# A decoder layer on one core: experts' down matrices split in two halves, a shorter staging ring, a slot table in PSUM, a new order of steps

## What is computed

```
# block 1: gated memory
gate = sigmoid(xn @ Wg + bg);  store = (xn @ Wv) * gate * scale
mem  = smear(store, 0.95)                      # a scan along the sequence
x    = x + (mem * sigmoid(xn @ Wq + bq) * scale) @ Wo
# block 2: attention over a context of 256 rows of 64
kv   = ctx @ W_k.T + b_k
sim  = (xn @ kv) @ kv.T / 16
x    = x + softmax(layernorm(sim) * gamma + beta)
# block 3: one of 8 experts per token, and a shared expert
idx, score = argmax(xn @ router_w), sigmoid(max(xn @ router_w))
for e in range(8): out += where(idx == e, (silu(xs @ gate_w[e]) * (xs @ up_w[e])) @ down_w[e], 0)   # xs = xn * score
x    = x + out + (silu(xn @ sh_gate) * (xn @ sh_up)) @ sh_down
```

## Time and profile before

| | us |
|---|---|
| runs shown | 143.40, 144.98, 147.16; median 144.98 |
| the profiled execution | 144.02, of which the span of the core's instructions 142.3 |
| busy in the span | PE 113.3 (80%), DVE 91.2 (64%), POOL 75.5 (53%), ACT 65.7 (46%) |
| mean granted clock of TensorE | 0.948 |
| DMA | 16.44 MB, mean 116 GB/s |
| chain that ended last | PE 65%, issue 11%, DVE 9%, POOL 4%, DMA 4%, ACT 3% |

### The profile page before, as it was taken

One profiled execution on the slowest core, in us unless ns is written; L12 is line 12 of the kernel. 1 busy time (PEld: TensorE's weight loads), 2 busy tenths in 40 slices (PEclk: granted clock), 3 DMA queues, 4 the chain that ended last, 5 costly groups with the idle time before them and its releaser, 6 DMA issues.

```text
span 142.3 us, 2530 instructions
## 1 busy us (share of the span) xinstructions
PE 113.3 (80%) x679; PEld 93.0 (65%) x679; DVE 91.2 (64%) x279; ACT 65.7 (46%) x169; POOL 75.5 (53%) x110
## 2 busy tenths in 40 slices
PE   0199999999899997968889301989999999999700
PEld 0169699687697894856769101757888888888400
DVE  2673995489999799799468998047554553643100
ACT  3335996936996347662350100034445444444300
POOL 5207069281894376556866992000446646646680
PEclk9999999999999999999999965589999999999985
DMA  4997984917047225002215702933254363243200
GB/s 130 242 277 170 368 264 105 280 60 223 0 134 244 72 72 149 0 7 78 78 39 193 245 0 50 316 126 77 78 89 79 81 91 61 29 48 37 29 1 0
DMA packets 18924, 16.44 MB, mean 116 GB/s; under 512 B 4320, under 2 KB 18656, under 8 KB 18912
## 3 DMA queue, kind: packets, MB, share of 16 engines
q1 hardware_dynamic: 15792, 13.56, 32.2%
q0 software_dynamic: 2544, 2.17, 9.2%
q10 hardware_dynamic: 576, 0.56, 1.1%
HBM read 11.82 MB, written 5.38 MB: 121 GB/s over the span
## 4 chain that ended last, share of the span: by engine, by line
PE 65%; issue 11%; DVE 9%; POOL 4%; DMA 4%; ACT 3%; SPq 1%; POOLq 0%; ACTq 0%
PE bG L876 15%; PE bQ L876 12%; PE bO L957 5%; PE bV L1083 4%; PE bV L876 4%; PE bO L1083 4%; DMA ez<-in_ctx_dram 4%; PE bU L965 3%; PE bV L1032 3%; PE bS L975 2%; POOL x_sorted L436 2%; PE bM L876 2%; PE bT L1054 1%; POOL out_dram L457 1%; PE bU L882 1%
## 5 line engine op out<-in xcount | busy, mean ns | idle before, releaser
L457 POOL DMA_INDIRECT out_dram<-tq,tid x15 | 23.3, 1552 | 29.0 <-DVE tid L846 26.3
L443 POOL TENSOR_TENSOR gu_lo<-stage,gu_hi 128x512 fp32r<-128x512 f32 x16 | 20.1, 1282 | 0.2
L1032 PE MATMUL bV<-shd,xn 128*128 128x256 f32 x32 | 9.5, 450 | 9.1 <-DVE xn L813 9.1
L1032 PEld LDWEIGHTS bV<-shd,xn 128*128 128x128 f32 x32 | 6.9, 225 | 10.5 <-issue 9.5
L436 POOL DMA_INDIRECT x_sorted<-xs,dest x8 | 8.4, 1056 | 5.1 <-issue 3.6
L409 POOL TENSOR_SCALAR vareps<-mv 128x2 f32<-128x2 f32 x8 | 2.0, 248 | 16.4 <-DVE mv L666 16.2
L663 DVE BATCH_NORM_STATS2 bn<-res 128x6 f32<-128x256 f32 x24 | 8.9, 414 | 2.3 <-DMA res<-in_x_dram 2.3
L612 ACT CAST xT_hi<-bT 128x256 fp32r<-128x256 f32 x8 | 2.9, 368 | 13.9 <-PE bT L1054 13.9
L493 ACT CAST gu_hi<-stage 128x512 fp32r<-128x512 f32 x16 | 9.3, 618 | 0.0
L474 ACT ACTIVATE xn<-res,shift,rstd 128x256 f32<-128x256 f32 x14 | 7.7, 596 | 3.5 <-POOL shift L417 3.5
L1083 PE MATMUL bV<-dn,xT 128*128 x32 | 8.3, 383 | 0.6 <-ACT xT L624 0.6
(11 more groups left out here) (190 smaller groups left out, 342.5 us busy)
## 6 DMA issues: line engine op xcount, KB each, us to landing
stage<-in_L_ffn_gate_w_dram SPq DMA_DIRECT2D x8, 256.0 KB, 3.5
stage<-in_L_ffn_up_w_dram SPq DMA_DIRECT2D x8, 256.0 KB, 3.3
dn<-in_L_ffn_down_w_dram SPq DMA_DIRECT2D x8, 256.0 KB, 3.5
xs<-x_sorted SPq DMA_DIRECT2D x15, 136.0 KB, 2.1
res<-in_x_dram SPq DMA_DIRECT2D x4, 256.0 KB, 3.5
out_dram<-res SPq DMA_DIRECT2D x4, 256.0 KB, 2.9
x_sorted<-pad SPq DMA_DIRECT2D x5, 136.0 KB, 2.9
x_sorted<-pad ACTq DMA_DIRECT2D x4, 136.0 KB, 3.0
```

The source lines that it names most:

```text
L443: g.tensor_tensor(units[n][2], stage[:, n % RING], f32(units[n][1]), ALU.subtract).then_inc(unit_lo, 1)
L457: g.indirect_dma_start(out_rows, bass.IndirectOffsetOnAxis(tid[:, s:s + 1], 0), ry[:, s % TILE_RING, :], None, bounds_check=N - 1, oob_is_ ...
L1032: last = T.matmul(psV[:, i, :], hs[:, b % 2, k, i * P:(i + 1) * P], shd[:, k, :], start=(k == 0), stop=(k == KT - 1))
```

## The change

Four things change. (1) `down_w` of each expert becomes a third unit of the ring, split into dn_hi and dn_lo: 29 units instead of 21, eight weight_hi more on ACT and eight weight_lo more on POOL, and no direct loads of dn. In the tile loop the hidden rows are split too (hidden_hi on ACT in place of the copy, hidden_lo new on DVE), and down becomes `product` with six matmuls of 256 columns. (2) RING goes from 6 to 4. (3) Four rows of the slot table (ntile, tile_s, te_f, and offset, formerly in tr_f) lie in a PSUM bank. (4) All four orders are laid out anew. A wait in weight_lo for the table is dropped; it belonged to a unit number that the old list didn't have.

```diff
 POOL_ORDER = """
-    rstd1:0 rstd1:1 rstd1:2 rstd1:3 weight_lo:3 weight_lo:4 sim_eps:0 weight_lo:5 weight_lo:6
-    sim_eps:3 rstd3:2 sim_rstd:3 scale_rows:1 scatter:0 rstd3:3 scatter:1 scale_rows:2 scatter:2
-    scale_rows:3 scatter:3 weight_lo:15 weight_lo:16 weight_lo:17 weight_lo:18 weight_lo:19
+    rstd1:0 rstd1:1 rstd1:2 rstd1:3 weight_lo:3 weight_lo:4 weight_lo:5 weight_lo:6 sim_eps:0
+    sim_eps:3 sim_rstd:3 rstd3:2 scale_rows:1 scatter:0 rstd3:3 weight_lo:23 weight_lo:24 scatter:1
+    scale_rows:2 scatter:2 scale_rows:3 scatter:3 weight_lo:25 weight_lo:26 weight_lo:27
...
     TILE_RING = 2 * KT
     ROUNDS = (NS - 3 - PEEL) // TILE_RING
-    RING = 6
+    RING = 4
     PROJ = 3
 
...
         gu_hi = sb("gu_hi", [P, E, KT, 2 * D], F32R)
         gu_lo = sb("gu_lo", [P, E, KT, 2 * D], F32R)
-        dn = sb("dn", [P, E, KT, D])
+        dn_hi = sb("dn_hi", [P, E, KT, D], F32R)
+        dn_lo = sb("dn_lo", [P, E, KT, D], F32R)
         kvT_all = sb("kvT_all", [C, B, S])
         kv_rows = sb("kv_rows", [P, B, KT, C])
...
-        ntile = sb("ntile", [1, E])
-        tile_s = sb("tile_s", [1, NS])
-        te_f = sb("te_f", [1, NS])
-        before = sb("before", [1, NS])
+        preceding = sb("preceding", [1, NS])
-        hT = xT2[:, :, :, 0:P]
+        hT_hi, hT_lo = xT1_hi[:, :, :, P:2 * P], xT1_lo[:, :, :, P:2 * P]
...
+        spare = 2 * TB * E
+
+        def ps_row(n):
+            nonlocal spare
+            spare += n
+            return bT[0:1, spare - n:spare]
+
+        ntile, tile_s, te_f, offset = ps_row(E), ps_row(NS), ps_row(NS), ps_row(NS)
-        small_in = {n: sem(f"{n}_in") for n in ("wk", "ctx", "bk", "bias", "wo", "gamma", "beta", "rw", "shd", "dn")}
+        small_in = {n: sem(f"{n}_in") for n in ("wk", "ctx", "bk", "bias", "wo", "gamma", "beta", "rw", "shd")}
...
         units += [(rows(w), shw_hi[:, i], shw_lo[:, i]) for i, w in enumerate((sh_gate_w, sh_up_w))]
         for e in range(E):
             units += [(rows(gate_w[e]), gu_hi[:, e, :, 0:D], gu_lo[:, e, :, 0:D]),
-                      (rows(up_w[e]), gu_hi[:, e, :, D:2 * D], gu_lo[:, e, :, D:2 * D])]
+                      (rows(up_w[e]), gu_hi[:, e, :, D:2 * D], gu_lo[:, e, :, D:2 * D]),
+                      (rows(down_w[e]), dn_hi[:, e], dn_lo[:, e])]
         SHARED_LO = 2
-        LAST_AFTER_TABLE = 26
 
         def f32(ap):
             return ap.bitcast(F32)
...
             sp.dma_start(x_sorted[E * REGION:E * REGION + P, :], pad[:, :]).then_inc(padded, 16)
             for n in range(PROJ, len(units)):
                 load_unit(n)
-                if n == PROJ + 1:
+                if n == RING:
                     load("shd", shd[:, :, :], rows(sh_down_w))
-                if n >= RING and (n - RING) // 2 < E and (n - RING) % 2 == 0:
-                    load("dn", dn[:, (n - RING) // 2], rows(down_w[(n - RING) // 2]))
-            for e in range((len(units) - RING + 1) // 2, E):
-                load("dn", dn[:, e], rows(down_w[e]))
 
             def store_base(b):
...
 
             def weight_lo(n):
                 pool.wait_ge(unit_hi, n + 1)
-                if n == LAST_AFTER_TABLE:
-                    pool.wait_ge(table_made, 1)
                 g.tensor_tensor(units[n][2], stage[:, n % RING], f32(units[n][1]), ALU.subtract).then_inc(unit_lo, 1)
 
             steps = {"rstd1": lambda b: rsqrt(LN1, b),
...
-            def hidden_copy(s, r, reused):
+            def hidden_hi(s, r, reused):
-                a.copy(hT[:, r], psH[r][:, :, 0:P]).then_inc(hT_made, 1)
+                a.copy(hT_hi[:, r], psH[r][:, :, 0:P]).then_inc(hT_hi_made, 1)
...
                     dve.wait_ge(table_step, step[0])
 
                 link(v.tensor_tensor(cmp_k[:, :, :], io_k[0:1, :, :], ps_count[0:1, :].unsqueeze(2).to_broadcast([1, E, NT]), ALU.is_lt))
-                link(v.tensor_reduce(ntile[:, :], cmp_k[:, :, :], AX.X, ALU.add))
-                link(v.tensor_tensor_scan(incl[:, :], one_e[:, :], ntile[:, :], 0.0, ALU.mult, ALU.add))
-                link(v.tensor_scalar(tile_s[:, :], io_s[:, :], incl[:, E - 1:E], None, ALU.min))
-
-                link(v.tensor_tensor(cmp_s[:, :, :], tile_s[:, :].unsqueeze(2).to_broadcast([1, NS, E]),
+                link(v.tensor_reduce(ntile, cmp_k[:, :, :], AX.X, ALU.add))
+                link(v.tensor_tensor_scan(incl[:, :], one_e[:, :], ntile, 0.0, ALU.mult, ALU.add))
+                link(v.tensor_scalar(tile_s, io_s[:, :], incl[:, E - 1:E], None, ALU.min))
+
+                link(v.tensor_tensor(cmp_s[:, :, :], tile_s.unsqueeze(2).to_broadcast([1, NS, E]),
                                      incl[:, :].unsqueeze(1).to_broadcast([1, NS, E]), ALU.is_ge))
-                link(v.tensor_reduce(te_f[:, :], cmp_s[:, :, :], AX.X, ALU.add))
-                link(v.tensor_tensor(cmp_s[:, :, :], cmp_s[:, :, :], ntile[:, :].unsqueeze(1).to_broadcast([1, NS, E]), ALU.mult))
-                link(v.tensor_reduce(before[:, :], cmp_s[:, :, :], AX.X, ALU.add))
-                link(v.tensor_tensor(tr_f[:, :], tile_s[:, :], before[:, :], ALU.subtract))
-                link(v.tensor_scalar(tr_f[:, :], tr_f[:, :], float(P), None, ALU.mult))
-                v.tensor_scalar(te[:, :], te_f[:, :], E - 1.0, None, ALU.min)
-                v.scalar_tensor_tensor(tr[:, :], te_f[:, :], float(REGION), tr_f[:, :], ALU.mult, ALU.add).then_inc(table_made, 1)
+                link(v.tensor_reduce(te_f, cmp_s[:, :, :], AX.X, ALU.add))
+                link(v.tensor_tensor(cmp_s[:, :, :], cmp_s[:, :, :], ntile.unsqueeze(1).to_broadcast([1, NS, E]), ALU.mult))
+                link(v.tensor_reduce(preceding[:, :], cmp_s[:, :, :], AX.X, ALU.add))
+                link(v.tensor_tensor(offset, tile_s, preceding[:, :], ALU.subtract))
+                link(v.tensor_scalar(tr_f[:, :], offset, float(P), None, ALU.mult))
+                v.tensor_scalar(te[:, :], te_f, E - 1.0, None, ALU.min)
+                v.scalar_tensor_tensor(tr[:, :], te_f, float(REGION), tr_f[:, :], ALU.mult, ALU.add).then_inc(table_made, 1)
 
             def shared_hidden(b):
...
 
+            def hidden_lo(s, r):
+                dve.wait_ge(hT_hi_made, s + 1)
+                v.tensor_tensor(hT_lo[:, r], psH[r][:, :, 0:P], f32(hT_hi[:, r]), ALU.subtract).then_inc(hT_lo_made, 1)
+
             rows_lo(0, 0, 0)
             rows_lo(1, 1, 1)
             hidden(0, 0)
             rows_lo(2, 0, 2)
             for s in range(PEEL):
                 hidden(s + 1, (s + 1) % 2)
+                hidden_lo(s, s % 2)
                 rows_lo(s + 3, (s + 1) % 2, (s + 3) % TILE_RING)
             with dve.Fori(0, ROUNDS) as i:
                 for j in range(TILE_RING):
                     s = i * TILE_RING + (PEEL + j)
                     r = (PEEL + j) % 2
                     hidden(s + 1, 1 - r)
+                    hidden_lo(s, r)
                     rows_lo(s + 3, 1 - r, (PEEL + j + 3) % TILE_RING)
             for s in range(PEEL + ROUNDS * TILE_RING, NS):
                 if s + 1 < NS:
                     hidden(s + 1, (s + 1) % 2)
+                if s < NS:
+                    hidden_lo(s, s % 2)
                 if s + 3 < NS:
                     rows_lo(s + 3, (s + 1) % 2, (s + 3) % TILE_RING)
...
                 if reused:
-                    pe.wait_ge(hT_made, s - 1)
+                    pe.wait_ge(hT_lo_made, s - 1)
                 for k in range(KT):
                     last = T.transpose(psH[r][:, k, 0:P], rh[:, r, k * P:(k + 1) * P], ident[:, :])
                 last.then_inc(th_done, 1)
 
             def down(s, r, e, reused):
-                pe.wait_ge(hT_made, s + 1)
+                pe.wait_ge(hT_lo_made, s + 1)
                 if reused:
                     pe.wait_ge(y_made, s - 1)
-                for k in range(KT):
-                    last = T.matmul(psY[r][:, 0, :], hT[:, r, k, :], dn[:, e, k, :], start=(k == 0), stop=(k == KT - 1))
-                last.then_inc(down_done, 1)
+                product(psY[r][:, 0, :], [(hT_hi[:, r, k, :], hT_lo[:, r, k, :], dn_hi[:, e, k, :], dn_lo[:, e, k, :])
+                                          for k in range(KT)]).then_inc(down_done, 1)
 
             pe.wait_ge(table_made, 1)
             e = experts(0, NS)
             pe.wait_ge(unit_lo, len(units) - PROJ)
-            pe.wait_ge(small_in["dn"], 16 * E)
             rows_turn(0, 0, 0, 1, False)
             rows_turn(1, 1, 1, 1, False)
             pe.wait_ge(sm["h_made"], B)
```

62 lines of the change are left out of this document (32 added, 30 removed).

## The result

| | before | changed |
|---|---|---|
| median, us | 144.82 (143.4 to 147.16, 4 runs) | 140.61 (139.75 to 140.62, 4 runs) |
| profiled execution, span | 142.3 | 138.5 |
| T, first row transposes | 91.56 | 89.30 |
| from T to the end | 50.7 | 49.2 |

The ratio is 0.9724, 95% interval 0.9656 to 0.9792: faster, but by 4.2 us where I had said 9.5 (144.98 to 135.5), and 0.1 us outside my range. (Ratios here leave disturbed runs out, medians don't, so the two can differ.) T is where PE starts on the first row transposes, in the kernel before with their weight load under the running shared_down (the matmul itself at 91.99). Of the two terms, T came 2.3 us earlier instead of 6.9, and the part behind T is 1.5 us shorter instead of 2.4.

A forecast was written before the change was run, and what follows sets the result against it. Bound: PE idle 9 us behind te, held on DVE by POOL; then POOL's last weight_lo. From 144.02 us: T -6.9, first transposes -0.4, tile loop -2.0, holds and clock +0.8, in sum -8.5: 135.5 us, range 131.5 to 140.5.

The forecast's parts named there:

- The table's rows in PSUM: On DVE ahead of T: te reading PSUM isn't held by POOL's run, 0.2 us instead of 7.93, saving 7.7 us.
- Rival 1: At te on DVE: the stall stays wherever te reads, T 88.8 to 90.6, 139.5 to 141 us; chance 0.12.
- What is late next, POOL: Ahead of T: POOL finishes last, rstd3:3 ends at 65.0 and the last weight_lo at 84.7, so T moves -6.9 us.
- rival 2: In the front: POOL's weight_lo hold kv_mean, centre_kv and residual3 on DVE, 1.3 to 5.1 us, 136 to 140; chance 0.18.
- holds and clock together: Term of +0.8 us for DVE held in longer weight_lo runs and for the clock behind PE's 3.5 us wait.
- Down in two halves: Tile loop: down takes 0.72 us instead of 0.86, -2.0 us over 14 periods; hidden_lo's latency is hidden.
- The 0.4 us for the first transposes: On PE at T: first transposes at full clock, 0.22 us a pair instead of 0.44, twice: -0.4 us.
- POOL's added 10.3 us: Eight more weight_lo at 1.28 us, said to fit in POOL's some 15 us of pauses and charged nothing.
- The own case: The forecast's main case: the stall goes, POOL sets T at 84.7, 135.5 us in all; chance 0.55.
- Rival 3: POOL's front: pauses stay unused, the 10.3 us come on top, T 96.6 and 147.0 us; chance 0.10.
- rival 4: PE-bound front: POOL finishes before PE, T at 81.2, 132 us; chance 0.05.
- What would show it: Signs: te 0.2, last weight_lo at 83 to 88, PE waiting about 3, period 2.55 us; wrong if turn_kv waits.

The follow-up runs named there:

- e1: The kernel before with only the slot table's rows put in PSUM: 140.97 us, ratio 0.9711.
- e5: The changed kernel with only the slot table's rows put back in SBUF: 146.68 us in one run.
- e9: The changed kernel with a probe behind its end: twelve times two scatters, six weight_lo, and te from SBUF at shifted starts; its time says nothing.
- e16: e14 with shared_hidden:0 left out but for two columns: similarity:3's start to rstd3:3's end stayed at 12.9 us; no total time given.
- e3: The changed kernel with sim_scale:3, destination:1 (DVE), softmax_exp:3 and score_tanh:2 (ACT) moved: 140.53 us.
- e8: The changed kernel with the edits of e2 and e3, and destination:0 directly behind sim_stats:3 on DVE: 138.19 us, ratio 0.9546.
- e10: e8 with route:1 back ahead of sim_scale:3 on DVE and destination:0 behind sim_stats:3: 139.65 us, ratio 0.9666.
- e2: The changed kernel with centre_kv reading PSUM and weight_lo:15 waiting for residual3:0, to remove two DVE holds: 138.89 us, ratio 0.9523.
- e7: e1 (down not split, six buffers) with weight_lo:15 to 18 moved from behind scatter:3 into POOL's pauses: 138.55 us.
- e15: The changed kernel with six staging buffers instead of four: 140.35 us, ratio 0.9734.
- e14: e2 with score_tanh:2 moved ahead of weight_hi:25 on ACT: 139.73 us, ratio 0.9528.

## Why the prediction was right or wrong

**The table's rows in PSUM**: right, and shown by e1 (5.1 us at T) with its ratio of 0.971. The reason I gave, a run of POOL instructions holding a DVE instruction that reads SBUF, is shown by the probes, but to the run's end only for a run that closely follows a scatter; without one it was held for one weight_lo. In the new order the rows weren't needed (e5). Rival 1 is out: PSUM ended the hold in all pieces. Its argument from `tr_f` has lost its force with e9: `tr_f` began 0.76 us ahead of the run, between the 0.65 that is held and the 0.87 that isn't, so where it began is enough to explain that it went through.

**What is late next, POOL**: right in kind (PE waits for the last weight_lo at T, with te, ring and DMA in time), wrong in size. The step that failed is "I count 1.5 to 2.3 us earlier, and take 2. Then rstd3:3 ends at 65.0". It ended 3.9 us later than that:
- 2.0 us: I took the way from similarity:3 to rstd3:3 as unchanged. It grew from 10.9 to 12.9 us. In both kernels rstd3:3 starts on POOL right behind scatter:0, scatter:0 waits for destination:0, and this stands on DVE behind sim_stats:3, route:1 and sim_scale:3. New between sim_stats:3 and sim_scale:3 is residual3:2, 1.9 us (58.36 to 60.29). Before (destination:0's end, rstd3:3's start), then after (residual3:2, and the same two):

```profile
61.61 0.17 DVE L780 CAST dest<-dest_f 128x2 uint32<-128x2 f32 x1
...
65.45 0.24 POOL L409 TENSOR_SCALAR vareps<-mv 128x2 f32<-128x2 f32 x1
...
58.53 0.88 DVE L751 SCALAR_TENSOR_TENSOR res<-ez,rsum,res 128x256 f32<-128x256 f32 x2
...
63.53 0.17 DVE L782 CAST dest<-dest_f 128x2 uint32<-128x2 f32 x1
...
67.29 0.24 POOL L413 TENSOR_SCALAR vareps<-mv 128x2 f32<-128x2 f32 x1
```

Counted from the start of similarity:3 (56.14 and 55.95), destination:0 ends after 5.64 us before and 7.75 us after; from there to rstd3:3's start it is 3.67 and 3.59 us. Less work on DVE ahead of similarity:3 didn't shorten it (e16). No run moved residual3:2, so that it alone costs the 2 us is read from the traces and not tested; e3, e8 and e10 moved steps around it, and each time another wait ended last (destination:0 still behind route:1; scale_rows:1 for the score of sequence 1; rstd3:2, 1.89 us for residual3:2). Which exchange would undo it is open: the exponentials that residual3:2 reads ended at 57.84 us, so it couldn't simply go back ahead of sim_stats:3.
- 1.3 us: the holds of rival 2, shown by e2. I had +0.8 for holds and clock together, with up to 5.1.
- 0.5 us: without the holds similarity:3 is 1.5 us earlier than before, not 2. This is less than executions differ by in where their steps lie, so it has no cause shown.

Behind rstd3:3 I had 19.7 us to the last weight_lo; it took 20.4. POOL waited 1.5 us for the score, which followed from half clock on PE, a cost that I had placed behind T alone. The rest of this way was 0.8 us shorter.

**Down in two halves**: right in the period (2.53 against 2.55, down 0.71 against 0.72) and in that nothing else bounds it. Wrong was "in the last tile it is hidden by POOL": PE waited 0.88 and 1.06 us for hidden_lo in the last tiles and the last down ran at half clock. From the start of the last gate_up to that of the last scatter it is 8.5 us (124.73 to 133.26) against 7.8 before (129.25 to 137.03): 0.7 us of the 2.0 lost. The 0.4 us for the first transposes came by half: they took 0.44 and 0.38 us instead of 0.64 and 0.63, and gate_up began 1.5 us behind them instead of 1.7.

**The sum**: -2.3 at T and -1.5 behind it make -3.8 in the span of the profiled executions (-3.4 in their times, 144.02 to 140.61), against -8.5. That POOL's added 10.3 us would hide was right for POOL itself, which still waited for DVE ahead of rstd3:3; their price was the time for which they held DVE. The own case, with rival 2's mechanism inside it, is what happened, at a time that the range missed by 0.1 us: the range had no room for an unpriced 2 us in a step that I took from before as it stood. **Rival 3** (147.0) and **rival 4** (PE as the bound) didn't occur.

**What would show it**: te 0.2 (0.16), unit_lo's last directly ahead of the transposes (yes, at 89.24 and not 83 to 88), PE waiting some 3 us (1.87), period 2.55 (2.53). turn_kv did wait 0.8 us, which I had named as a sign of being wrong; it was worth 0.5.

## What to carry to other kernels

When a stall is removed, the next bound has to be taken from the new order, not from the old timeline: count every instruction that now stands between two points of the chain, on each engine, before calling their distance unchanged. None of the DVE instructions tried here that read PSUM in place of SBUF was held by GpSimd, so small control data can go there if a scatter and long GpSimd work come next; an order in which it is read earlier did the same (e5). Work moved into an engine's pauses is free only up to the point where its own output is waited for: behind the last scatter about 5 us were free here, while four weight_lo (5.0 us) moved ahead of it made it 1.8 us later (e7).

## What the runs showed of the hardware

- A DVE instruction from SBUF beside six back-to-back GpSimd tensor_tensor waits for one of them (1.22 to 1.3 us), but behind an indirect DMA issued by GpSimd just before, until all six are over (7.15 to 8.05 us, in 11 starts from 0.65 us ahead of their displayed start to 0.24 us inside; the twelfth, 0.87 us ahead, was not held). The Trainium skill (SBUF — State Buffer, section Who interferes with whom) gives the pair to whoever issues first "for the whole instruction"; without a scatter the trace agrees, behind one the measured hold is longer, and the measurement decides.
- Alike waits of PE were followed by half clock in the changed kernel, in both its traces (0.53 and 0.55 from 68.8 to 72.4 us), and by full clock in e15 and e2; what differs I could not find. It is worth 1.4 us here (e15), and in the profiled execution of e14 2 us behind T.
- A short hold can just move: with centre_kv reading PSUM, the 64x2 instruction ahead of it took 1.12 us.
